# Second root stage of a graph network: two small row statistics move from VectorE to GpSimd

## What is computed

```python
def _layernorm(x, axis=-1, eps=1e-05):
    m = jnp.mean(x, axis=axis, keepdims=True)
    v = jnp.var(x, axis=axis, keepdims=True)
    return (x - m) / jnp.sqrt(v + eps)
...
            agg = jax.ops.segment_sum(msg, row, num_segments=x.shape[0])
            return agg + x @ root + bias
...
    x = x + _L0_gnn_ref(_layernorm(x, axis=-1), edge_index, edge_type_2, ...)
    x = x + _L0_ffn_ref(_layernorm(x, axis=-1)[None], ...)[0]
```

## Time and profile before

| | us |
|---|---|
| median of 3 runs | 4586.38 |
| lowest, highest | 4577.79, 4600.59 |
| the profiled execution | 4589.7 |
| its span | 4587.9 |
| second root stage, share of that span | about 292 |

### The profile page before, as it was taken

One profiled execution on the slowest core, in us unless ns is written; L12 is line 12 of the kernel. 1 busy time (PEld: TensorE's weight loads), 2 busy tenths in 40 slices (PEclk: granted clock), 3 DMA queues, 4 the chain that ended last, 5 costly groups with the idle time before them and its releaser, 6 DMA issues. The chain is left out here.

```text
span 4587.9 us, 64995 instructions
## 1 busy us (share of the span) xinstructions
PE 4069.8 (89%) x22652; PEld 3302.0 (72%) x22652; DVE 2832.4 (62%) x5495; ACT 2040.4 (44%) x3505; POOL 1400.9 (31%) x1391
## 2 busy tenths in 40 slices
PE   7978999889979268689999999998899998999967
PEld 3447788777768156549988579986699874998844
DVE  5665666669976667467854445543455444557888
ACT  1223233323346033265567533475433764335566
POOL 1442266228810048654410323101332004330010
PEclk9988999999999578779999999999899998999965
DMA  8985487549989159864423555324654237444677
GB/s 309 402 319 180 167 293 252 176 161 386 393 294 317 27 135 175 142 215 155 155 85 111 196 178 161 102 95 154 217 159 126 86 117 241 157 157 138 185 196 212
DMA packets 462789, 886.21 MB, mean 193 GB/s; under 512 B 73189, under 2 KB 113750, under 8 KB 461711
## 3 DMA queue, kind: packets, MB, share of 16 engines
q1 hardware_dynamic: 300347, 527.00, 33.7%
q0 software_dynamic: 90016, 237.51, 18.5%
q10 hardware_dynamic: 72136, 117.94, 7.2%
HBM read 609.61 MB, written 303.62 MB: 199 GB/s over the span
## 5 line engine op out<-in xcount | busy, mean ns | idle before, releaser
L2057 POOL DMA_INDIRECT hidden_agg<-edge_sums,edge_where x316 | 354.7, 1123 | 697.0 <-DVE layer_raw_inner L2144 284.7
L783 PE MATMUL hidden_O<-hidden_xh,layer_hi_inner 128*128 128x256 f32 (+1 forms) x1280 | 367.2, 287 | 0.2 <-DVE hidden_xl L1183 0.2
L785 PE MATMUL hidden_O<-hidden_xl,layer_hi_inner 128*128 128x256 f32 (+1 forms) x1280 | 361.3, 282 | 0.0
L784 PE MATMUL hidden_O<-hidden_xh,layer_lo_inner 128*128 128x256 f32 (+1 forms) x1280 | 360.6, 282 | 0.0
L1902 POOL DMA_INDIRECT message_x<-g,edge_partner x120 | 117.5, 979 | 776.8 <-POOLq L150 458.2
L2101 ACT ACTIVATE hT_inner<-hidden_O,hidden_b 128x256 f32<-128x256 f32 (+1 forms) x320 | 124.1, 471 | 333.6 <-PE hidden_O L785 333.6
L783 PE MATMUL root_O<-root_hi,root_xh 128*128 128x512 f32 (+1 forms) x632 | 254.0, 402 | 13.8 <-DVE root_xl L1183 13.8
L783 PE MATMUL output_O<-layer_hi_inner,output_hh 128*128 128x512 f32 (+1 forms) x632 | 250.2, 396 | 0.1
L785 PE MATMUL output_O<-layer_lo_inner,output_hh 128*128 128x512 f32 (+1 forms) x632 | 249.6, 395 | 0.0
L784 PE MATMUL output_O<-layer_hi_inner,output_hl 128*128 128x512 f32 (+1 forms) x632 | 249.6, 395 | 0.0
L2247 DVE TENSOR_TENSOR layer_raw_inner<-output_O,output_b2t 128x1024 f32<-128x1024 f32 x80 | 96.9, 1211 | 246.4 <-PE output_O L785 246.4
(11 more groups left out here) (491 smaller groups left out, 12429.8 us busy)
## 6 DMA issues: line engine op xcount, KB each, us to landing
edge_sums<-message_res SPq DMA_DIRECT2D x160, 256.0 KB
layer_raw_inner<-g SPq DMA_DIRECT2D x78, 512.0 KB, 4.2
g<-layer_raw_inner SPq DMA_DIRECT2D x78, 512.0 KB
room<-in_L_gnn_basis SPq DMA_DIRECT2D x30, 1280.0 KB, 13.7
order_basis<-in_L_gnn_basis SPq DMA_DIRECT2D x18, 1280.0 KB, 14.3
edge_sums<-relation_res SPq DMA_DIRECT2D x82, 256.0 KB
order_x<-in_x SPq DMA_DIRECT2D x39, 512.0 KB
normed<-order_y ACTq DMA_DIRECT2D x39, 512.0 KB
```

What stands on the lines that cost most here:

```text
L783: eng.matmul(out, a_hi, b_hi, start=start, stop=False)
L784: eng.matmul(out, a_lo, b_hi, start=False, stop=False)
L785: return eng.matmul(out, a_hi, b_lo, start=False, stop=stop)
L2057: eng.indirect_dma_start(agg[j % R][0:n, :], None, ed.sums[1], bass.IndirectOffsetOnAxis(ap=ed.where[1][0:n, c:c + 1], axis=0)).then_inc(g ...
```

## The change

DVE ends each group at the two bn_aggr, which now signal `aggr`. POOL waits for `aggr`, computes the negated mean into `ng` and the variance plus epsilon into `mv`, and goes on with its power as before. DVE also gets a wait for `nb` of three groups earlier in front of bn_stats, since POOL now reads what the aggregates write.

```diff
                 def rstd(g):
                     q = g % S
                     n, k = (REST, 1) if last(g) else (P, TILES)
+                    eng.wait_ge(s["aggr"], g + 1)
+                    eng.tensor_scalar(ng[q][0:n, 0:k], mv[q][0:n, 0:k, 0], -1.0, None, ALU.mult)
+                    eng.tensor_scalar(mv[q][0:n, 0:k, 1], mv[q][0:n, 0:k, 1], EPS, None, ALU.add).then_inc(s["var"], 1)
                     wait(eng, s["norm"], g - S + 1)
                     row_rstd(eng, s, g, mv[q], half, rs[q], last(g))
...
                     eng.wait_ge(s["y"], g + 1)
-                    row_stats(eng, s, g, y[q], bn[q], mv[q], o, ng[q])
+                    wait(eng, s["nb"], g - S + 1)
+                    for t, n in tiles_of(o):
+                        m = eng.bn_stats(bn[q][0:n, t, :], y[q][0:n, t, :])
+                    m.then_inc(s["stats"], 1)
+                    eng.wait_ge(s["stats"], g + 1)
+                    for t, n in tiles_of(o):
+                        m = eng.bn_aggr(mv[q][0:n, t, :], bn[q][0:n, t, :])
+                    m.then_inc(s["aggr"], 1)
```

## The result

The changed kernel takes **4621.5 us** (median of 6 runs, 4611.7 to 4641.6) against 4588.2 of the kernel before (6 runs, 4577.8 to 4600.6): ratio **1.0094**, 95% interval 1.0074 to 1.0113. The prediction was 4581.6 us with a range to 4606.

A forecast was written before the change was run, and what follows sets the result against it. VectorE was taken to set the stage's 6.98 us period. Its saving of up to 10.5 us, limited by the DMA engines to 4.8, with 0 elsewhere, took the median from 4586.4 to 4581.6 us; range 4572 to 4606.

The forecast's parts named there:

- VectorE's saving: On VectorE, aggregates to xl falls from 0.43 to 0.16 us: 0.27 us a group, at most 10.5 us over 39 groups.
- The price of the two operations: On GpSimd, two tensor_scalar at 0.20 us each plus a self-wait of 0.08: +0.48 us a group.
- the need itself: GpSimd's work per group without holds, 6.03 us before, rising to 6.51, under VectorE's new period of 6.71.
- The holds: GpSimd stalls during VectorE operations with two SBUF inputs: 0.95 us a group before, most of the added 0.48 going into them.
- It may slide: GpSimd may run later against VectorE until its starts fall better, with 0.20 us a group left for holds.
- The late norm on ACT: On ACT, rs and nb are ready 2.5 us before being read; a late norm first eats ACT's own idle time.
- GpSimd becomes the bound: Rival, chance 0.20: GpSimd's need plus holds exceeds the period of 6.98 us; 4610 to 4629 us, or +9 us mildly.
- t over 0.34: On GpSimd, t is one new operation's price in us; the bound moves there if 6.31 + 2t exceeds 6.98.
- The DMA engines: In the stage, if they move no more than now, stores of y limit the gain to 4.8 us; chance 0.40.
- The library instruction: On GpSimd, it occurs once, in the fourth turn, and was taken as 0 us.
- The stage's end: After the last group, the power slips by about 0.15 us but is hidden behind ACT: 0 us.

The follow-up runs named there:

- experiments 2: Kernel before, VectorE unchanged, with the two operations and a self-wait added on GpSimd into buffers nothing reads: 4581.5 us, ratio 1.0008.
- experiment 7: Changed kernel with a wait for the aggregates and two tensor_scalar that nothing reads added on VectorE: 4589.2 us, ratio 1.0025 to the kernel before.
- experiment 4: Changed kernel with ACT's norm one turn later (lag 4 instead of 3): timed 4593.0 us, ratio 1.0032 to the kernel before.
- experiment 1: Changed kernel with negation and epsilon left out on both engines: 4573.9 us, ratio 0.9993 to the kernel before.
- experiment 9: Changed kernel with negation and epsilon left out on both engines and SyncE's load of skp a turn later: 4568.5 us, ratio 0.9971.
- experiments 6: Changed kernel, epsilon left out on both engines: 4597.3 us, ratio 0.9980; or epsilon kept on VectorE, negated mean on GpSimd: 4598.6 us, ratio 0.9991.

## Why the prediction was wrong

*VectorE's saving*: right. 0.27 us forecast, 0.29 measured (6.98 to 6.69), aggregates to `xl` 0.16 us.

*The price of the two operations* is the first step that failed. The term had 0.20 us each and 0.08 for a self-wait, + 0.48. The duration was nearly right, 0.22 to 0.23, but a queue pays from start to start: 0.30 + 0.37 = 0.67 where 0.48 was counted, and 0.04 more between the last gather and the first of them. The same reading by durations was wrong in the need itself: the first gather was taken at 0.96 us once the holds were out, and it is 1.11 behind `nb` in the unheld rows. So 6.03 + 0.48 = 6.51 should have been 6.03 + 0.15 + 0.71 = **6.89**, and that isn't under 6.71. The prediction knew that start to start is what counts and used it for VectorE; on GpSimd it didn't.

*The holds.* "It may slide" is the second step that failed. Where the period is longer than its need GpSimd does slide to a place where it is hardly held (experiments 2 and 7). Where its need is over VectorE's period it doesn't settle, and the sliding itself costs holds, 1.14 us a group; the prediction let holds fall with the slide. The Trainium skill calls the pair of SBUF ports that the two engines share an exclusive lock, held for a whole instruction ("SBUF — State Buffer", section SBUF: two separate sides). The rows agree: the power that began 0.12 us into L1146 ended 0.58 us behind it.

*The late norm on ACT*: the step that cost most. "A late norm on ACT first eats ACT's own idle time" is right, and the cover was larger than the 2.5 us that the prediction read: 8 us until VectorE is touched. It was taken as enough without a count of how fast it goes, 1.34 us a group, and of what stands behind it: `xh`, in the same queue, for which VectorE waits. From group 11 on VectorE is tied to GpSimd. By experiment 4 the place of that tie is 24 of the 34.9 us.

*The rival "GpSimd becomes the bound"* is what happened, with chance 0.20 and 4610 to 4629, and 4621 lies in it; but not by its own rule. It wanted t over 0.34, and t is 0.30 to 0.37. The point of decision was set against the old period of 6.98; it is the new period of 6.69 that GpSimd has to keep, and the change lowered that at the same time as it raised the need.

The Trainium skill's advice against elementwise work on GpSimd ("GPSIMD Engine Reference", section Engine selection), which the prediction set aside as meant for large tiles, pointed the right way. But its row gives no tile size, and it says about twice VectorE's time for operations with two inputs and roughly the full rate for those with one, as the two moved ones are. That isn't what was measured: on 128x2 it was 0.30 and 0.37 us against 0.06 and 0.08.

*The DMA engines.* Size right, -4.8 against -4.3 in experiment 1 and -7.4 in experiment 9; the place wrong in the first (loads of `xin`, by SyncE's order) and right in the other. It had no bearing on the changed kernel, which moves 332 GB/s.

*The library instruction*: 0 was right; on the changed kernel's GpSimd the first small operation starts at 1034.13 as soon as the aggregates are there, and the one behind it 0.30 us later. The about 6 us that the Trainium skill gives for loading code ("GPSIMD Engine Reference", section Instruction dispatch) are not seen here; whether this instruction loads any isn't shown. *The stage's end* can't be judged: nothing there is hidden behind the same work any more.

**What stays open.** That the place of VectorE's restart fixes the holds, so that a group takes 8.3 us on the mean in the changed kernel and 7.27 in experiment 4, is read from the rows and the sums of the holds of these two; why the holds fall as they do in each isn't worked out. That the slide would have been harmless without holds is an estimate. Why GpSimd had its one gap of 0.45 us in experiment 7 isn't known.

## What to carry to other kernels

When work moves from the engine that sets the period to one that seems to have room, compare the receiver's need from start to start, with gaps, with the period after the change, not before it; a margin of 0.1 us held here and one of -0.2 us cost 35 us in 34 groups. Idle time of the receiver hidden as holds is real spare time only as long as it keeps up; once it doesn't, holds add to what it falls back by, here 1.14 us to 0.20. Then count how late the moved result may be before the busy engine waits, and ask what stands behind its consumer in that in-order queue. If the aim is just to take a wait off the busy engine, moving the two small operations behind the next large one on the same engine shortened the 34 periods by 3.4 us, though the whole kernel's time didn't change measurably.

## What the runs showed of the hardware

A tensor_scalar of 128x2 on GpSimd lasts 0.22 us, and its successor starts 0.30 to 0.37 us after its start; on VectorE the same two cost 0.06 and 0.08 us from start to start. An indirect gather's issue is 0.96 us, 1.11 directly behind a small operation. A hold by a VectorE operation adds up to nearly that operation's length: 0.96 us to a power of 0.73, 0.84 to a gather of 1.11. What it adds to a group is no constant: the same power took 0.73, 0.79 or 1.21 us on the mean in experiments 6 and 7 and in the changed kernel.
